# Moving the transposed scores one slot later and giving each value product its own slot in a fused FFN–attention–FFN kernel

## The chip, the cores and the metric

One core of one Trainium2 chip runs the whole kernel. The metric is the time of one execution on the device in microseconds (us). Lower is better.

## What is computed

The input X is 16 sequences of 256 rows by 128 columns. Three residual blocks follow each other:

```
x = x + 0.5 * ffn(layernorm(x))     # FP4-quantised activations and weights, 128 -> 352 -> 128, silu(gate) * up
x = x + attention(layernorm(x))     # 16 heads of 8, causal softmax, @ Wo + bo
x = x + 0.5 * ffn(layernorm(x))
```

In the attention, for each head, `A = softmax(Q K^T / sqrt(8), causal)` and `Y = A V`.

## The kernel before

**Stages.** The first FFN runs over the 16 sequences, then the attention, then the second FFN. Each is a software pipeline: iteration `it` (called a *turn* here) works on sequence `it - lag` at each step, by the table `ATT_LAG`, and all engines issue their share of the steps in the one order of `ATT_ORDER`. The attention has turns 0 to 22. Turns 0 to 4 are woven into the first FFN. Turns 5 to 7 and 16 to 19 are written out with the full order (`FULL`; in 18 and 19 the steps of sequences past the last fall away), turns 8 to 15 are a loop unrolled by four, and the rest, the tail, is woven by hand with the second FFN (`ATT_TO_FFN`, L113 to L124).

**Steps of one sequence.** `lnS lnA lnE lnN` is the layernorm (VectorE, GpSimd, then ScalarE). `xT`, copied by `xTc` (ScalarE, L754), is the transposed input; `qk` (TensorE, L1245) projects queries and keys. `c1`, `split`, `c2` and `third` cut them into three bf16 parts; `third` is a GpSimd subtraction (L604), `c2` a ScalarE cast (L764). `stack` stores the parts to DRAM and loads them back as stacks (SyncE's DMA queue). `v` is the value projection, copied by ScalarE (L772).

`S0` to `S11` (TensorE, L1268) are the scores, each one PSUM bank, and VectorE takes row maxima of each (L1050). `nmS` (VectorE, L1059 to L1065) splits the negated maxima in three parts. `nm` transposes them (TensorE, L1278), ScalarE copies them (L779), and a DMA puts them into the query stack (`load_nm`, L506).

`ST0` to `ST11` (TensorE, L1299) are the transposed scores with the maxima already subtracted. They alternate between the banks `st0` and `st1`. ScalarE takes the exponential of each (L790), GpSimd zeroes the upper triangle (the mask, L619). `ST0` waits for the DMA of the maxima. Three ST make up a group of four heads.

`AV0` to `AV3` (TensorE, L1326 and L1330, 128x32 weights, four heads side by side in the 128 columns) multiply one group each by the values. `AVg` waits for the mask of `ST(3g+2)`; the even ones also wait until the bank `ot0` is empty. `oc0` copies it after AV1, `oc1` after AV3 (ScalarE, L800). `oT0 oT1`, `n0 n1` (VectorE, L1073 and L1075), `yT`, `yTc` (ScalarE, L809), `wo` (TensorE, L1356) and `wa` normalise, transpose and project.

**Slots.** I call slot k of a turn the stretch of the order around `Sk`. One ST stands in each slot too. Each engine takes its steps strictly in the order, so a step that waits holds everything behind it on its engine.

The waits of the exponential and of the value product:

```python
if not first(b, 1):
    act.wait_ge(filled["AV"], GROUPS * (b - 1) + g + 1)          # exp(c): group's probs read by the sequence before
nc.scalar.activation(probs[:, c, :], ps[:, :], ACT.Exp, scale=SCALE).then_inc(done, 1)

pe.wait_ge(taken["AV"], PAIRS * b + pair)                        # attend(g), even g only
pe.wait_ge(masked, CHUNKS * b + 3 * g + 3)                       # attend(g), every g
```

Of the kernel before, what the change touches and what calls it, by code (L numbers as in the profile page):

```python
# [77 lines left out]
    "third stack v",  # L78
    "",
    "S0 S1 S2 S3 S4 S5 S6 S7 S8 S9 S10 S11",  # L80
    "nmS nm ST0 ST1 ST2 ST3 ST4",
    "ST5 ST6 ST7 ST8 ST9 ST10 ST11 AV0 AV1 AV2 AV3 oc0 oc1",
    "oT0 oT1 n0 n1 yT yTc wo wa sS sA sE",
)) for step in steps.split()}
ATT_ORDER = """
nmS ST5 S0 oT0 third  ST6 n0 S1  ST7 nm lnN S2 stack  ST8 S3 oT1 n1 AV0 AV1 bias
ST9 oc0 xT S4  ST10 xTc lnS S5 yT  yTc ST11 lnA S6  ST0 lnE S7 wo qk c1
ST1 wa S8  ST2 split S9 AV2 AV3  ST3 c2 oc1 sS S10 v  ST4 sA S11 sE
""".split()
ATT_UNROLL = 4  # L90
PART_TURNS = 2
# [16 lines left out]
FULL = " ".join(ATT_ORDER)  # L108
FFN_TO_ATT = [(13, None, FFN_TURN), (14, 0, WARM), (15, 1, WARM), (16, 2, WARM), (17, 3, WARM), (18, 4, FIRST_SCORES),
              (19, None, FIRST_REST), (20, None, REST_TRANSPOSES), (21, 4, REST_SCORES), (None, 1, "bias"), (None, 2, "bias"),  # L110
              (None, 3, "bias"), (None, 4, "bias"), (None, 5, FULL), (None, 6, FULL), (None, 7, FULL)]
LAST_PROBS = "nmS ST5 oT0 n0  ST6 nm f.xq  ST7 oT1  ST8  ST9 n1  ST10  ST11 AV0 yT f.xr"
LAST_RESIDUAL = "f.lnN  ST0  ST1 AV1 oc0 yTc  ST2 AV2  ST3  ST4 AV3 wo f.xq oc1 wa sS sA sE"  # L113
LAST_VALUES = """
ST5  ST6 f.xT  ST7 oT0 n0  ST8  ST9 AV0  ST10  ST11 f.xr f.gu0 AV1 f.gu1 oT1 n1 oc0 yT yTc AV2 AV3 f.h0 wo f.h1 wa oc1
"""
SECOND_GATES = "f.xT f.xq f.gu0 oT0 f.gu1 f.hq n0 f.xr f.h0 f.h1 f.hr f.lnN"
# [1 line left out]
THIRD_PRODUCTS = "f.xr f.h0 f.h1 f.hr f.lnN yT"  # L119
FOURTH_GATES = "f.hT0 f.xT f.hT1 f.xq f.gu0 yTc f.gu1 wo f.dn0 f.hq wa"  # L120
FOURTH_PRODUCTS = "f.xr f.h0 sS f.h1 sA sE f.hr f.lnN f.dn1"
ATT_TO_FFN = [(0, 16, FULL.replace("ST4", "f.lnN ST4")), (1, 17, FULL.replace("ST4", "f.lnN ST4")), (None, 18, FULL), (None, 19, FULL),
              (1, 20, LAST_PROBS), (2, 20, LAST_RESIDUAL), (2, 21, LAST_VALUES), (3, 22, SECOND_GATES),
              (4, 22, THIRD_GATES), (None, 21, "sS sA sE"), (4, 22, THIRD_PRODUCTS), (5, 22, FOURTH_GATES), (5, 22, FOURTH_PRODUCTS)]  # L124
VECTOR_COPIES = {"oc0": (14, 15), "oc1": (14,), "yTc": (13, 14), "f.xT": (0,)}
WOVEN_THIRDS = 3
# [116 lines left out]
def all_phases(eng, ffn1, att, ffn2, last, done=0):  # L243
# [5 lines left out]
    att.loop(eng)  # L249
    weave(ffn2, att, ATT_TO_FFN)  # L250
    ffn2.loop(eng)
# [6 lines left out]
def weave(ffn, att, turns):  # L258

    woven = set()
    for ffn_it, att_it, order in turns:
        for name in order.split():
            pipeline, it, step = (ffn, ffn_it, name[2:]) if name.startswith("f.") else (att, att_it, name)
            if it is not None and 0 <= it - pipeline.lag[step] < pipeline.batches:
                assert (pipeline is ffn, it, step) not in woven
                woven.add((pipeline is ffn, it, step))
                pipeline.step(step, it, it)
    for pipeline, n in ((ffn, 0), (att, 1)):  # L270
        for it in {turn[n] for turn in turns} - {None}:
            for step, lag in pipeline.lag.items():
                assert (pipeline is ffn, it, step) in woven or not 0 <= it - lag < pipeline.batches, (it, step)
# [1118 lines left out]
```

## Time and profile before

| | us |
|---|---|
| median of 3 runs | 486.52 |
| lowest, highest | 481.95, 491.36 |
| profiled execution, its own time | 480.36 |
| its span | 478.6 |
| TensorE busy | 390.8 (82%) |
| VectorE busy | 417.0 (87%) |
| ScalarE busy | 317.4 (66%) |
| GpSimd busy | 259.1 (54%) |

The profiled execution lies 6.2 us below the median. 1.8 us of it lie outside the span. The attention's full turns fill about 160 to 343 us of the span, the first FFN what lies before, the second what lies behind. Busy shares are averages over the three stages; a busy TensorE matmul row contains the latency of a pipelined matmul, so gaps between starts say more than busy time.

### The profile page before, as it was taken

The numbers are of one execution on the slowest core, as the hardware profiler recorded it, in microseconds if no ns is written. First come the engines' busy times: TensorE is split into PE (matmuls) and PEld (weight loads), VectorE is DVE, ScalarE is ACT, GpSimd is POOL, SyncE is SP. The second block draws the span as 40 slices with busy tenths as digits, with TensorE's granted clock in tenths as the row PEclk, the third lists the DMA queues.
The fourth block names the chain that finished last, engine by engine and source line by source line (L and its number), as shares of the span: only waits on it lengthen the run. The fifth ranks groups of instructions, "written<-read, shape, count | busy, mean of one in ns | idle before, by whom it ended". The sixth has DMA issues, their size and how long they took to land.

```text
span 478.6 us, 12396 instructions
## 1 busy us (share of the span) xinstructions
PE 390.8 (82%) x3433; PEld 285.9 (60%) x3433; DVE 417.0 (87%) x1132; ACT 317.4 (66%) x861; POOL 259.1 (54%) x479
## 2 busy tenths in 40 slices
PE   0558888887886899998999999988895778888886
PEld 0325665665574567676767767666553556656665
DVE  3788999998888879998999998878868999999994
ACT  3557888777651767777778777776773456656643
POOL 6455666645525457776777776656671242233321
PEclk9988999998899789999999999999999889999999
DMA  7887000000445444445554445440000000000001
GB/s 215 239 132 134 4 0 0 1 1 17 131 144 146 141 125 127 127 123 148 149 149 131 130 135 147 137 140 21 7 1 1 2 12 23 22 22 22 22 12 44
DMA packets 38440, 39.30 MB, mean 82 GB/s; under 512 B 1789, under 2 KB 35453, under 8 KB 36093
## 3 DMA queue, kind: packets, MB, share of 16 engines
q1 hardware_dynamic: 38397, 38.79, 30.5%
q8 instruction: 20, 0.33, 0.3%
q14 instruction: 23, 0.19, 0.1%
HBM read 21.91 MB, written 10.49 MB: 68 GB/s over the span
## 4 chain that ended last, share of the span: by engine, by line
PE 42%; issue 23%; DVE 10%; ACT 10%; POOL 8%; DMA 5%; POOLq 0%; ACTq 0%; DVEq 0%; SPq 0%
PE bank L1299 7%; PE bank L1326 6%; PE bank L1268 5%; DMA q_stack<-nmT 4%; PE bank L1159 4%; PE bank L1160 3%; PE bank L1188 3%; POOL hq_out L551 3%; PE bank L1245 3%; PE bank L1330 3%; ACT probs L790 2%; PE bank L1356 2%; POOL fln_rstd L577 1%; PE bank L1146 1%; PE bank L1179 1%
## 5 line engine op out<-in xcount | busy, mean ns | idle before, releaser
L1050 DVE TENSOR_REDUCE nm<-bank 128x2 f32<-128x512 f32 (+1 forms) x192 | 126.6, 682 | 20.6 <-PE bank L1268 18.3
L790 ACT ACTIVATE probs<-bank 128x512 f32<-128x512 f32 x192 | 108.7, 608 | 38.2 <-PE bank L1299 37.2
L619 POOL TENSOR_SCALAR_AFFINE_SELECT probs<-probs 128x256 f32<-128x256 f32 (+1 forms) x192 | 90.3, 485 | 59.0 <-ACT probs L790 56.9
L1299 PE MATMUL bank<-q_stack,k_stack 75*128 75x256 bf16 (+1 forms) x512 | 74.1, 248 | 9.8 <-ACT probs L790 5.0
L1268 PE MATMUL bank<-k_stack,q_stack 127*128 127x256 bf16 (+1 forms) x512 | 74.3, 250 | 1.5 <-DVE nm L1050 1.5
L551 POOL TENSOR_TENSOR xq_out<-xq_grid,xq_scale 128x256 f32<-128x256 bf16 x32 | 24.4, 762 | 76.5 <-DVE xq_grid L894 76.5
L1159 PE MATMUL bank<-wguT,f_xT 128*128 128x352 f32 x128 | 57.5, 534 | 6.3 <-ACT f_xT L713 4.3
L1299 PEld LDWEIGHTS bank<-q_stack,k_stack 75*128 75x128 bf16 x512 | 37.3, 97 | 29.4 <-ACT probs L790 13.7
L1188 PE MATMUL bank<-wdT,f_hT 128*128 128x128 f32 (+1 forms) x384 | 53.4, 275 | 1.4 <-ACT f_hT L731 1.4
L720 ACT ACTIVATE f_silu<-bank 128x352 f32<-128x352 f32 x64 | 29.3, 458 | 37.1 <-PE bank L1160 37.0
L1188 PEld LDWEIGHTS bank<-wdT,f_hT 128*128 128x128 f32 (+1 forms) x384 | 49.9, 191 | 6.5 <-ACT x_all L705 0.9
L1160 PE MATMUL bank<-wguT,f_xT 128*128 128x352 f32 x128 | 53.4, 501 | 0.0
L551 POOL TENSOR_TENSOR hq_out<-hq_grid,hq_scale 128x704 f32<-128x704 bf16 x31 | 42.8, 1382 | 10.8 <-DVE hq_grid L894 10.8
L1268 PEld LDWEIGHTS bank<-k_stack,q_stack 127*128 127x128 bf16 x512 | 41.2, 99 | 7.6 <-DVE nm L1050 2.9
L1146 PE MATMUL bank<-ident,xq_out 128*128 128x128 f32 x64 | 14.5, 311 | 37.5 <-POOL xq_out L551 22.2
L1326 PE MATMUL bank<-probs,v_stack 128*32 128x256 f32 x512 | 41.1, 393 | 0.2 <-DVE oT L1090 0.2
L1015 DVE TENSOR_TENSOR f_h<-f_silu,bank 128x352 f32<-128x352 f32 x64 | 32.6, 515 | 4.9 <-ACT f_silu L720 4.7
L1160 PEld LDWEIGHTS bank<-wguT,f_xT 128*128 128x128 f32 x128 | 26.9, 210 | 16.1 <-issue 4.5
L1159 PEld LDWEIGHTS bank<-wguT,f_xT 128*128 128x128 f32 x128 | 23.3, 208 | 20.7 <-ACT f_xT L713 14.3
L1179 PE MATMUL bank<-ident,hq_out 128*128 128x128 f32 (+1 forms) x192 | 32.4, 278 | 3.8 <-ACT f_hT L731 3.8
L1146 PEld LDWEIGHTS bank<-ident,xq_out 128*128 128x128 f32 x64 | 6.8, 146 | 45.8 <-POOL xq_out L551 26.9
L729 ACT COPY f_hT<-bank 128x256 f32<-128x256 f32 x64 | 23.8, 372 | 5.6 <-PE bank L1179 5.4
(149 smaller groups left out, 876.4 us busy)
## 6 DMA issues: line engine op xcount, KB each, us to landing
q_stack<-q_parts SPq DMA_DIRECT2D x16, 576.0 KB
k_stack<-k_parts SPq DMA_DIRECT2D x16, 576.0 KB
q_parts<-qk_parts SPq DMA_DIRECT2D x16, 192.0 KB, 2.1
k_parts<-qk_parts SPq DMA_DIRECT2D x16, 192.0 KB, 2.4
v_stack<-zeros_bf SPq DMA_DIRECT2D x1, 2048.0 KB, 10.1
k_parts<-qk_parts SPq DMA_DIRECT2D x16, 128.0 KB, 2.3
out_dram<-x_all SPq DMA_DIRECT2D x15, 128.0 KB, 1.8
q_stack<-mask_q SPq DMA_DIRECT2D x1, 1664.0 KB
```

The lines of the kernel that those rows point to most:

```text
L551: nc.gpsimd.tensor_tensor(q.out[:, s, :].rearrange("p (n k) -> p n k", k=BLOCK), q.grid[:, s, :].rearrange("p (n k) -> p n k", k=BLOCK), q ...
L619: nc.gpsimd.affine_select(out=v, in_=v, compare_op=ALU.is_ge, fill=0.0, base=0, pattern=[[0, heads], [1, P]], channel_multiplier=-1).then_ ...
L790: nc.scalar.activation(probs[:, c, :], ps[:, :], ACT.Exp, scale=SCALE).then_inc(done, 1)
L1015: nc.vector.tensor_tensor(f_h[:, j, :], f_silu[:, j, :], ps.up[j][:, 0:I], ALU.mult).then_inc(h_ready[j], 1)
L1050: nc.vector.tensor_reduce(nm[:, j, h0:h0 + n], ps[:, :].rearrange("p (h k) -> p h k", h=n), AX_X, ALU.max, negate=True).then_inc(done, 1)
L1159: nc.tensor.matmul(ps.gate[j][:, 0:I], x, wguT[:, 0, :], start=True, stop=True)
L1160: nc.tensor.matmul(ps.up[j][:, 0:I], x, wguT[:, 1, :], start=True, stop=True).then_inc(gu_filled[j], 1)
L1179: last = nc.tensor.transpose(ps.hT[0:k, P * t:P * t + P], hquant.out[:, s, I * j + P * t:I * j + P * t + k], ident[:, :])
L1188: nc.tensor.matmul(out, f_hT[0:k, t, P * j:P * j + P], wdT[0:k, t, :], start=(t == 0), stop=False)
L1268: last = nc.tensor.matmul(ps[:, keys * h:keys * h + keys], q_stack[0:ROWS, s, h0 + h, P * j:P * j + P], k_stack[0:ROWS, s, h0 + h, 0:keys] ...
L1299: last = nc.tensor.matmul(ps[:, w * n:w * n + w], k_stack[0:SROWS, s, HG * g + h, k0:k0 + P], q_stack[0:SROWS, s, HG * g + h, q0:T], start ...
L1326: nc.tensor.matmul(ps[VW * h:VW * h + VW, 0:T], window(s, 0, h), probs[:, slot + h // 2, T * (h % 2):T * (h % 2) + T], start=(half == 0), ...
```

## The change

All steps stay, with the same shapes, buffers and waits. Three things move:

- Every ST stands one slot later. Slot 0 now has ST4 and not ST5, and so on to slot 7 with ST11; ST0 stands in slot 8 and not 7, behind `wo`, `qk` and `c1`. ST4 moves to the lag of ST5.
- The value products stand alone: AV0 stays in slot 3, AV1 goes behind S4, AV2 behind S8, AV3 stays behind S9. `oc0` goes from slot 4 to slot 5, behind `xTc` and ahead of `yTc`.
- In the tail one more ST (ST4 of sequence 14) stands behind the last maxima; `LAST_RESIDUAL` is cut in two around ST4 of the last sequence, in the same order.

```diff
-    "nmS nm ST0 ST1 ST2 ST3 ST4",
-    "ST5 ST6 ST7 ST8 ST9 ST10 ST11 AV0 AV1 AV2 AV3 oc0 oc1",
+    "nmS nm ST0 ST1 ST2 ST3",
+    "ST4 ST5 ST6 ST7 ST8 ST9 ST10 ST11 AV0 AV1 AV2 AV3 oc0 oc1",
...
-nmS ST5 S0 oT0 third  ST6 n0 S1  ST7 nm lnN S2 stack  ST8 S3 oT1 n1 AV0 AV1 bias
-ST9 oc0 xT S4  ST10 xTc lnS S5 yT  yTc ST11 lnA S6  ST0 lnE S7 wo qk c1
-ST1 wa S8  ST2 split S9 AV2 AV3  ST3 c2 oc1 sS S10 v  ST4 sA S11 sE
+nmS ST4 S0 oT0 third  ST5 n0 S1  ST6 nm lnN S2 stack  ST7 S3 oT1 n1 AV0 bias
+ST8 xT S4 AV1  ST9 xTc oc0 lnS S5 yT  yTc ST10 lnA S6  ST11 lnE S7 wo qk c1
+ST0 wa S8 AV2  ST1 split S9 AV3  ST2 c2 oc1 sS S10 v  ST3 sA S11 sE
...
-LAST_PROBS = "nmS ST5 oT0 n0  ST6 nm f.xq  ST7 oT1  ST8  ST9 n1  ST10  ST11 AV0 yT f.xr"
-LAST_RESIDUAL = "f.lnN  ST0  ST1 AV1 oc0 yTc  ST2 AV2  ST3  ST4 AV3 wo f.xq oc1 wa sS sA sE"
+LAST_PROBS = "nmS ST4 ST5 oT0 n0  ST6 nm f.xq  ST7 oT1  ST8  ST9 n1  ST10  ST11 AV0 yT f.xr"
+LAST_SCORES = "f.lnN  ST0  ST1 AV1 oc0 yTc  ST2 AV2  ST3"
+LAST_RESIDUAL = "AV3 wo f.xq oc1 wa sS sA sE"
...
-ATT_TO_FFN = [(0, 16, FULL.replace("ST4", "f.lnN ST4")), (1, 17, FULL.replace("ST4", "f.lnN ST4")), (None, 18, FULL), (None, 19, FULL),
-              (1, 20, LAST_PROBS), (2, 20, LAST_RESIDUAL), (2, 21, LAST_VALUES), (3, 22, SECOND_GATES),
+ATT_TO_FFN = [(0, 16, FULL.replace("ST3", "f.lnN ST3")), (1, 17, FULL.replace("ST3", "f.lnN ST3")), (None, 18, FULL), (None, 19, FULL),
+              (1, 20, LAST_PROBS), (2, 20, LAST_SCORES), (None, 21, "ST4"), (2, 20, LAST_RESIDUAL), (2, 21, LAST_VALUES), (3, 22, SECOND_GATES),
```

## Rows read from the trace of the kernel before

**Rows 1.** The page: busy time, share, instructions.
```profile
PE 390.8 (82%) x3433; PEld 285.9 (60%) x3433; DVE 417.0 (87%) x1132; ACT 317.4 (66%) x861; POOL 259.1 (54%) x479
```
**Rows 2.** Chain that ended last, whole run: start, us, what (`qk`, turns 6, 8, 9, 16).
```profile
174.31 0.86 PE bank L1245 x4
...
199.55 0.87 PE bank L1245 x4
...
211.98 0.87 PE bank L1245 x4
...
301.07 0.87 PE bank L1245 x4
```
**Rows 3.** The same chain inside turns 8 and 9, ST3 to ST6.
```profile
202.74 0.34 PE bank L1299 x2
...
204.63 0.63 ACT probs L790
...
205.31 0.39 PE bank L1299 x2
```
**Rows 4.** Timeline of TensorE, turn 9: start, us, line, shapes [idle before].
```profile
207.38 0.64 PE L1326 MATMUL bank<-probs,v_stack 128*32 128x256 f32 x8
207.84 0.40 PE L1330 MATMUL bank<-probs,v_stack 128*32 128x128 f32 x8
208.06 0.61 PE L1326 MATMUL bank<-probs,v_stack 128*32 128x256 f32 x8
208.49 0.40 PE L1330 MATMUL bank<-probs,v_stack 128*32 128x128 f32 x8
208.82 0.39 PE L1299 MATMUL bank<-q_stack,k_stack 75*128 75x256 bf16 x2
...
210.97 0.39 PE L1268 MATMUL bank<-k_stack,q_stack 127*128 127x256 bf16 x2
211.30 0.68 PE L1356 MATMUL bank<-wqkvo,yT 128*128 128x128 f32 x4
```
**Rows 5.** Timeline of TensorE, turn 8, around AV2.
```profile
200.92 0.38 PE L1268 MATMUL bank<-k_stack,q_stack 127*128 127x256 bf16 x2
201.23 0.64 PE L1326 MATMUL bank<-probs,v_stack 128*32 128x256 f32 x8
```
**Rows 6.** Timeline of ScalarE, turn 9: exp of ST9, `oc0`, exp, `xTc`, `yTc`.
```profile
209.25 0.60 ACT L790 ACTIVATE probs<-bank 128x512 f32<-128x512 f32 x1 [0.84 <-PE bank L1299]
209.74 0.37 ACT L800 COPY oT<-bank 128x256 f32<-128x256 f32 x1
210.00 0.61 ACT L790 ACTIVATE probs<-bank 128x512 f32<-128x512 f32 x1
210.49 0.39 ACT L754 COPY a_xT<-bank 128x256 f32<-128x256 f32 x1
210.74 0.41 ACT L809 COPY yT<-bank 128x256 f32<-128x256 f32 x1
```
**Rows 7.** Timeline of GpSimd, turn 9: mask of ST5, `third`, masks of ST6 to ST8.
```profile
206.99 0.64 POOL L619 TENSOR_SCALAR_AFFINE_SELECT probs<-probs 128x512 f32<-128x512 f32 x1
207.59 1.17 POOL L604 TENSOR_TENSOR qk_parts<-qk_rest,qk_parts 128x512 bf16<-128x512 f32 x1
208.70 1.36 POOL L619 TENSOR_SCALAR_AFFINE_SELECT probs<-probs 128x256 f32<-128x256 f32 x3
```
**Rows 8.** Timeline of VectorE, turn 9: row maxima of S4.
```profile
209.69 0.69 DVE L1050 TENSOR_REDUCE nm<-bank 128x2 f32<-128x512 f32 x1 [0.45 <-PE bank L1268]
```
**Rows 9.** Waits: who for whom, us in total, times, longest us.
```profile
PE bank L1299 <- DMA q_stack<-nmT: 4.4, 5, 1.5
```
**Rows 10.** Timeline of TensorE, ST0 of turns 17 and 18.
```profile
314.25 0.38 PE L1299 MATMUL bank<-q_stack,k_stack 75*128 75x256 bf16 x2 [1.47 <-DMA q_stack<-nmT]
...
326.33 0.38 PE L1299 MATMUL bank<-q_stack,k_stack 75*128 75x256 bf16 x2 [0.71 <-DMA q_stack<-nmT]
```
**Rows 11.** Timeline of ScalarE in the tail: copy of the last sequence's maxima.
```profile
344.30 0.37 ACT L779 COPY nmT<-bank 48x256 bf16<-48x256 bf16 x1 [0.63 <-PE bank L1278]
```

## Prediction, made before the changed kernel was run

> **What bounds the kernel now.** I read the page first: VectorE is the busiest engine, 87%, TensorE 82% [rows 1]. That alone would make VectorE the bound, and the change would look like a relief for it, because its maxima of S4 wait 0.45 us each turn behind the pair AV0, AV1 [rows 8]. So I read the chain that ended last. It comes back to `qk` on TensorE in every turn, and from turn 6 to turn 16 it takes 301.07 - 174.31 = 126.76 us for ten turns [rows 2]. The undisturbed turn is 211.98 - 199.55 = 12.43 us [rows 2]. Ten of those are 124.3, so 2.46 us of the ten are disturbance.
>
> Inside a turn the chain leaves TensorE once: ST3 (202.74), its exponential, `c2`, `oc1`, `v`'s copy, the exponential of ST4 (204.63), and ST6, which needs that bank, at 205.31 [rows 3]. These 2.6 us are ScalarE's. The other 9.8 us are TensorE instruction behind instruction. VectorE isn't on the chain; its 0.45 us is slack.
>
> Disturbance comes from the DMA of the maxima: ST0 waited for it five times, 4.4 us together, 1.5 at most [rows 9]: 1.47 in turn 17, 0.71 in 18 [rows 10], the others in turns 6 to 16.
>
> **The change, part by part.** I walk through a turn with the gaps between starts of rows 4 to 7 and ask at each moved step what it now stands behind.
>
> *ST0 a slot later (gain).* Behind S7, `wo` and `qk` it runs some 1.9 us later (S7 at 210.97, `qk` at 211.98 and its 0.87 [rows 2, 4]), and the delays below add to it. The longest wait was 1.5 [rows 9], so all five go. In the ten turns that is 2.46 us. In 17 and 18 it is 1.47 + 0.71, less 0.1 or so that the next wait swallowed: 2.05. Together -4.5 us. Bounds: 0 if the load is late by something that moves along, -4.6.
>
> *Value products alone (loss).* A pair: AV0 takes 0.46 + 0.22 until AV1 starts, AV1 0.43 + 0.33 until ST9 starts [rows 4]. A score group of 256 columns otherwise starts 0.22 after the instruction before; so leaving the 128x32 products costs 0.11. Entering costs 0.09: S9 starts at 200.92, its two matmuls take 0.22, AV2 starts at 201.23 [rows 5]. The first group of a run takes 0.03 more. Each split adds one way in and one way out: 0.23 us. Two a turn, on the part of the chain that is TensorE's: 0.46. Over the 28 pairs of turns 6 to 19, 6.4 us. Bounds: 0, if the gaps are the price of AV's semaphore waits and the second of a pair, with one wait, has none; 28 x 0.33 = 9.2, if a split costs as much as the whole stretch from the last products to ST9. I take 0.23 because the way out shows at ST9, which has the one bank wait of every other ST.
>
 Without the rule the gaps could be waits and the term could be 0; the rule gives no duration.
>
> *AV1 behind `third` (loss).* AV1 needs the mask of ST5. Before, GpSimd did that mask (206.99) ahead of `third` (207.59) [rows 7]. Now the mask of ST4 stands there and the mask of ST5 behind `third`: 206.99 + 0.38 (ST4's mask, half as large) + 1.11 (`third`, 207.59 to 208.70) + 0.64 = 209.12, and 0.05 to TensorE, as from the exponential's end (204.63 + 0.63) to ST6 at 205.31 [rows 3]: 209.17. Without it AV1 would start at 207.38 + 0.79 (AV0 and the way out) + 3 x 0.22 (ST8, `xT`, S4) + 0.09 = 208.93. TensorE waits 0.24, and everything behind AV1 with it. `third` runs in turns up to 17: 11 x 0.24 = 2.6 us. Bounds: 0 (if ST4's mask and `third` start earlier) and 0.5 a turn.
>
> *`oc0` between ST9's exponential and `yTc` (loss).* On the scale without the wait of AV1, ST9 starts at 208.93 + 0.79 = 209.72. Its exponential starts 0.43 later (208.82 to 209.25 [rows 4, 6]), then 0.49, `xTc` 0.25, `oc0` 0.26 [rows 6]: `yTc` starts at 211.15, ends at 211.56, and `wo` can start at 211.61. TensorE would be there at 209.72 + 7 x 0.22 (ST9 to S7) + 0.11 (S7 at 210.97 to `wo` at 211.30, less 0.22 [rows 4]) = 211.37. It waits 0.24. Before, `yTc` ended at 211.15, ahead of `wo` at 211.30. Turns 7 to 16: 2.4. Turns 17 to 19 have no `xTc`, I take half: 0.4. Together 2.8 us. Bounds 0 and 0.35 a turn.
>
> *What stays.* The ScalarE stretch of 2.6 us begins at the ST of slot 10, which stands behind both AV2 and AV3 as before; its length is the same. S4 comes 0.7 us earlier; VectorE gains slack there that nobody waits for. At S9, one AV earlier in the queue than before, VectorE has `wa` and `split` to do. AV2 and AV3 wait for masks of slots 4 and 7, over a microsecond old. No DMA is added. `stack` waits for the last ST of four sequences earlier, now a slot later, but its stores release it later still.
>
> *Both ends.* Turn 5 loses one ST, 0.22 us, ahead of its maxima, at most; I count 0. In the tail one more exponential stands ahead of the copy of the last maxima; ScalarE was idle 0.63 us there [rows 11], an exponential is 0.5: 0.
>
> *Sum.* 6.4 + 2.6 + 2.8 - 4.5 = +7.3, less 0.3 for splits of turns 18 and 19 where VectorE may end the wait: +7.0. The full turn goes from 12.43 to 12.43 + 0.46 + 0.24 + 0.24 = 13.4 us, even in all turns. On the profiled execution's 480.36: 487.4 us.
>
> The median lies 6.2 us above that execution. In the trace, all unevenness of the turns is the load of the maxima, so I hold most of the 6.2 for more such waits, which go too. I let 0.6 us of them stand: **488 us**.
>
> **Rivals.**
>
> *The switches cost nothing.* If the gaps are semaphore waits, they fall away: 488 - 6.1 = 482 us. For it: `wo` too starts 0.11 late without a switch. Against: ST9 behind AV1, above.
>
> *The load of the maxima is the larger part, and the change is faster.* Place: ST0, every turn. In the median run these waits would be 4.5 + 6.2 = 10.7 us, all hidden now. With the other costs at 0 that gives 486.5 - 10.7 = 476; with a VectorE that was the bound after all, another 0.45 a turn for 13 turns, 470. It decides once the waits removed exceed the costs added by 9.7 us. For it: the spread of the runs, 481.95 to 491.36, and VectorE's 87%. Against: the order puts three new things behind queues, and the chain shows VectorE off it.
>
> *The waits add up.* All costs at their upper bounds: 9.2 + 11 x 0.5 + 13 x 0.35 = 19.3, less 4.5, is +15, and if the 6.2 us have nothing to do with the maxima: 486.5 + 15 = 501 us. Against: a wait on TensorE gives ScalarE and GpSimd time to catch up, so the two waits can't both be at their largest.
>
> **How the numbers follow.** Forecast 0.56, free switches 0.21, faster 0.10, adding up 0.13. The forecast has 484 to 494 for itself (0 or all of the 6.2 standing, and the mask wait at 0 or 0.5). With the free switches the range becomes **480 to 496**. A measurement of this kernel can tell about 2% from no change, 476.8 to 496.2 us. Faster by over 2%: 0.09, from its rival. Slower by over 2%: 0.15, from the waits that add up and a little of the forecast. Within 2%: 0.76.
>
> **What would show it.** Turns of 13.1 to 13.4 us, all alike; no wait of L1299 for the maxima; twice as many short idles before L1326; new waits of L1326 for the mask (L619) in slot 4 and of L1356 for `yT` (L809); VectorE's wait at S4 gone and its idle time elsewhere. Wrong would be turns below 12.43 (then VectorE was the bound), splits without gaps, or a wait at ST0 that stays.

## The result, and the profile after

| | before | after |
|---|---|---|
| median, executions side by side | 484.69 us (20) | 487.75 us (20) |
| lowest, highest | 481.74, 491.36 | 485.33, 489.65 |
| profiled execution, its span | 480.36, 478.6 | 488.02, 486.3 |
| `qk` of turn 6 to `qk` of turn 16 | 126.8 us | 133.6 us |

The changed kernel takes 1.0076 times the time of the kernel before, interval 1.0055 to 1.0097: slower by 0.8%, within the 2% and 0.25 us from the forecast. Medians here and below are over all executions; the ratios leave out those over 1.5% above the fastest of their kernel, which the kernel before has more often than the changed one, so a ratio can lie above the quotient of the medians. In the changed kernel's own line numbers every line named below is one higher than before.

The page of the changed kernel, busy time by engine, hardly differs from [rows 1]:

```profile
PE 396.6 (82%) x3433; PEld 282.2 (58%) x3433; DVE 416.6 (86%) x1132; ACT 319.8 (66%) x861; POOL 258.7 (53%) x479
```

The chain that ended last tells more. Its `qk` rows (start, us, what), turns 8 to 11:

```profile
197.76 0.87 PE bank L1246 x4
211.08 0.86 PE bank L1246 x4
224.40 0.87 PE bank L1246 x4
237.72 0.86 PE bank L1246 x4
```

A turn is now 13.32 us where it was 12.43 [rows 2]. Nine of the ten turns lie between 13.21 and 13.35 us; one is 13.79. Before, they went from 12.42 to 13.45.

TensorE's timeline of the changed kernel, turn 9 (start, us, line, shapes, [idle before]), from S4 to AV1, ST9 and on to S7, `wo`, `qk` and ST0:

```profile
207.08 0.38 PE L1269 MATMUL bank<-k_stack,q_stack 127*128 127x256 bf16 x2
207.62 0.64 PE L1327 MATMUL bank<-probs,v_stack 128*32 128x256 f32 x8 [0.15 <-POOL probs L620]
208.07 0.40 PE L1331 MATMUL bank<-probs,v_stack 128*32 128x128 f32 x8
208.41 0.39 PE L1300 MATMUL bank<-q_stack,k_stack 75*128 75x256 bf16 x2
...
209.74 0.39 PE L1269 MATMUL bank<-k_stack,q_stack 127*128 127x256 bf16 x2
210.40 0.68 PE L1357 MATMUL bank<-wqkvo,yT 128*128 128x128 f32 x4 [0.27 <-ACT yT L810]
210.91 1.03 PE L1246 MATMUL bank<-a_xT,wqk 128*128 128x256 f32 x4
211.78 0.38 PE L1300 MATMUL bank<-q_stack,k_stack 75*128 75x256 bf16 x2
```

AV1 starts 0.54 us after S4, where a value product behind scores starts 0.31 after them [rows 5]: 0.23 us is the wait for the mask behind `third`. `wo` starts 0.66 after S7, 0.33 before [rows 4]. ST0 follows `qk` without a gap. So a turn is 12.43 + 0.46 (two splits) + 0.23 (mask) + 0.33 (`yT`) - 0.14 (a gap that ST0 used to have) = 13.31 us.

ScalarE's timeline shows why `wo` waits: `oc0` (L801) stands between `xTc` and `yTc` (L810).

```profile
208.84 0.60 ACT L791 ACTIVATE probs<-bank 128x512 f32<-128x512 f32 x1 [1.18 <-PE bank L1300]
209.33 0.37 ACT L755 COPY a_xT<-bank 128x256 f32<-128x256 f32 x1
209.58 0.39 ACT L801 COPY oT<-bank 128x256 f32<-128x256 f32 x1
209.85 0.41 ACT L810 COPY yT<-bank 128x256 f32<-128x256 f32 x1
```

The waits of the changed kernel (who for whom, us in total, times, longest):

```profile
DVE nm L1051 <- PE bank L1269: 23.9, 48, 1.5
...
PEld bank L1327 <- issue: 8.3, 42, 0.2
PEld bank L1327 <- POOL probs L620: 6.0, 17, 0.6
...
PE bank L1357 <- ACT yT L810: 2.7, 10, 0.3
```

There is no row of a transposed score (L1300) waiting for the maxima's DMA, where before there was one of 4.4 us [rows 9].

**Where the 7.66 us between the two profiled executions went.** First FFN -1.15, turns 5 and 6 -1.96, the ten turns +6.81, the rest of the attention +0.42, the first turns of the second FFN +3.58, all else -0.04. The +6.81 and the +0.42 are where the attention's order moved; the others are taken up behind the experiments.

### The profile page after: what moved, and what is told of

The parts are those of the page before. It is cut to its first block, busy times and chain, and to the rows that moved or that the text cites. A ratio compares the mean times of both kernels' runs of the same rounds, so it can differ in the third digit from the quotient of the medians.

```text
span 486.3 us, 12396 instructions
## 1 busy us (share of the span) xinstructions
PE 396.6 (82%) x3433; PEld 282.2 (58%) x3433; DVE 416.6 (86%) x1132; ACT 319.8 (66%) x861; POOL 258.7 (53%) x479
## 4 chain that ended last, share of the span: by engine, by line
PE 41%; issue 24%; ACT 12%; DVE 10%; POOL 10%; ACTq 1%; DMA 1%; POOLq 1%; DVEq 0%
PE bank L1300 7%; PE bank L1327 6%; PE bank L1160 4%; PE bank L1269 4%; PE bank L1161 3%; PE bank L1189 3%; POOL hq_out L552 3%; PE bank L1246 3%; ACT probs L791 3%; PE bank L1331 2%; PE bank L1357 2%; ACT oT L801 2%; PE bank L1147 1%; POOL probs L620 1%; POOL fln_rstd L578 1%
## 5 line engine op out<-in xcount | busy, mean ns | idle before, releaser
L1051 DVE TENSOR_REDUCE nm<-bank 128x2 f32<-128x512 f32 (+1 forms) x192 | 127.5, 684 | 25.3 <-PE bank L1269 23.9
L791 ACT ACTIVATE probs<-bank 128x512 f32<-128x512 f32 x192 | 109.9, 606 | 41.3 <-PE bank L1300 40.8
L1300 PE MATMUL bank<-q_stack,k_stack 75*128 75x256 bf16 (+1 forms) x512 | 74.1, 249 | 7.1 <-ACT probs L791 7.0
L1300 PEld LDWEIGHTS bank<-q_stack,k_stack 75*128 75x128 bf16 x512 | 35.5, 98 | 28.8 <-ACT probs L791 13.4
L1327 PE MATMUL bank<-probs,v_stack 128*32 128x256 f32 x512 | 40.9, 391 | 1.8 <-POOL probs L620 1.4
L872 DVE SCALAR_TENSOR_TENSOR hq_normed<-f_h,hq_inv 128x704 f32<-128x704 f32 x31 | 27.3, 880 | 0.1
```

Source lines behind the costliest of these rows:

```text
L1051: nc.vector.tensor_reduce(nm[:, j, h0:h0 + n], ps[:, :].rearrange("p (h k) -> p h k", h=n), AX_X, ALU.max, negate=True).then_inc(done, 1)
L1300: last = nc.tensor.matmul(ps[:, w * n:w * n + w], k_stack[0:SROWS, s, HG * g + h, k0:k0 + P], q_stack[0:SROWS, s, HG * g + h, q0:T], start ...
L1327: nc.tensor.matmul(ps[VW * h:VW * h + VW, 0:T], window(s, 0, h), probs[:, slot + h // 2, T * (h % 2):T * (h % 2) + T], start=(half == 0), ...
```

## The experiments

"Turn" is the undisturbed turn, "ten turns" the time from `qk` of turn 6 to `qk` of turn 16, "load waits" those of ST0 on the maxima's load over the whole run, turns 17 and 18 included. The ratio is to the kernel before, timed side by side (its medians there were 483.45 to 485.61), and is what compares kernels of different rows. No ratio is 2% away from 1, though the intervals of x1, x3 and y3 reach past that; where an interval contains 1, no difference is shown. A turn's time counts from its `qk` to the next. Each trace is one execution.

| kernel | turn | ten turns | load waits | median | ratio |
|---|---|---|---|---|---|
| before | 12.43 | 126.75 | 4.4 | | 1 |
| changed | 13.32 | 133.57 | 0 | 487.75 | 1.0076 [1.0055, 1.0097] |
| x1_extra_waits | - | 133.64 | 12.4 | 485.77 | 1.0118 [0.9981, 1.0256] |
| x2_split_only | 12.80 | 132.38 | 3.9 | 483.82 | 1.0009 [0.9959, 1.0058] |
| x3_third | 13.09 | 131.69 | 2.0 | 487.33 | 1.0129 [1.0027, 1.0231] |
| x4_ytc | 13.04 | 130.82 | 0 | 484.14 | 1.0028 [0.9972, 1.0083] |
| x5_third_ytc | 12.81 | 129.64 | 4.5 | 486.37 | 1.004 [0.9994, 1.0086] |
| x6_pairs | 12.85 | 132.15 | 5.8 | 490.23 | 1.0114 [1.0047, 1.0182] |
| x7_c2 | 12.85 | 131.75 | 5.8 | 487.46 | 1.0052 [1.0011, 1.0093] |
| x8_c2_nm | 13.33 | 135.09 | 0 | 487.07 | 1.0062 [1.0023, 1.0101] |
| y1_wait_moved | 12.43 | 126.09 | 1.2 | 480.7 | 0.9874 [0.981, 0.9938] |
| y2_after_wait | 13.32 | 133.59 | 0 | 486.15 | 1.0071 [1.0045, 1.0097] |
| y3_pairs_wait | 12.48 | 125.52 | 0 | 477.85 | 0.9844 [0.9788, 0.99] |
| y4_pairs_xt | 12.48 | 130.19 | 6.6 | 486.24 | 1.0036 [0.9996, 1.0077] |

### Are the gaps around the value products waits?

**x1_extra_waits**, the kernel before with satisfied semaphore waits added:

```diff
+    if half == 1:
+        if not first(b, 1):
+            pe.wait_ge(taken["AV"], PAIRS * b)
+        pe.wait_ge(taken["v"], b + 1)
     pe.wait_ge(masked, CHUNKS * b + 3 * g + 3)
...
     if c == 0:
         pe.wait_ge(nm_loaded, 16 * (b + 1))
+    if c in (3, 9):
+        pe.wait_ge(nm_loaded, 16 * (b + 1))
```

> The kernel before, with two more waits that are already satisfied ahead of AV1 and AV3 and one more ahead of ST3 and ST9; order and work are the same. Theory (the gaps round the 128x32 products are the change of tiling, not the price of waits): AV1 still starts 0.22 us behind AV0's last products, ST9 still 0.33 behind AV1's, the undisturbed turn stays at 12.43 us (at most +0.1), ratio to before 1.000 within 0.003. Rival (the gaps are what semaphore waits cost): about 0.1 us more ahead of AV1 and AV3 and behind AV3 and AV1, so +0.3 to +0.5 us a turn and +4 to +6 us in all, ratio 1.008 to 1.013.

Measured, on TensorE's timeline of this kernel:

```profile
259.20 0.64 PE L1332 MATMUL bank<-probs,v_stack 128*32 128x256 f32 x8
259.65 0.40 PE L1336 MATMUL bank<-probs,v_stack 128*32 128x128 f32 x8
259.87 0.61 PE L1332 MATMUL bank<-probs,v_stack 128*32 128x256 f32 x8
260.30 0.40 PE L1336 MATMUL bank<-probs,v_stack 128*32 128x128 f32 x8
260.64 0.39 PE L1301 MATMUL bank<-q_stack,k_stack 75*128 75x256 bf16 x2
```

AV0's last group to AV1 is 0.22 us and AV1's last group to ST9 0.34, as in [rows 4] (0.22 and 0.33). Satisfied waits cost nothing there. The gap belongs to the change between 128x32 weights and the others. The element type, which changes at the same places, is not it: `v` (fp32) starts 0.22 us behind a bf16 score (203.12 behind 202.90 in the kernel before), and in the later y3_pairs_wait `xT` (fp32, 128x128) starts 0.34 behind the fp32 products of AV1 (216.91 behind 216.57).

The time itself says little. The ratio, 1.0118, lies where the rival had it, but its interval contains 1, and the medians are 485.77 and 485.32. The turn of 12.43 could not be read, since ST0 waited for the load in nine of the ten turns (turn 6, without a wait, took 12.54 us in both kernels); the profiled execution has three times the load waits of the kernel before, whose order it shares.

**x2_split_only**, the kernel before with AV1 behind S4, AV2 behind S8, and `oc0` behind `yTc`; no transposed score moves.

```diff
-nmS ST5 S0 oT0 third  ST6 n0 S1  ST7 nm lnN S2 stack  ST8 S3 oT1 n1 AV0 AV1 bias
-ST9 oc0 xT S4  ST10 xTc lnS S5 yT  yTc ST11 lnA S6  ST0 lnE S7 wo qk c1
-ST1 wa S8  ST2 split S9 AV2 AV3  ST3 c2 oc1 sS S10 v  ST4 sA S11 sE
+nmS ST5 S0 oT0 third  ST6 n0 S1  ST7 nm lnN S2 stack  ST8 S3 oT1 n1 AV0 bias
+ST9 xT S4 AV1  ST10 xTc lnS S5 yT  yTc oc0 ST11 lnA S6  ST0 lnE S7 wo qk c1
+ST1 wa S8 AV2  ST2 split S9 AV3  ST3 c2 oc1 sS S10 v  ST4 sA S11 sE
```

> The kernel before with the value products apart (AV1 behind S4, AV2 behind S8, AV3 behind S9) and oc0 behind yTc, where it holds up nothing; the transposed scores stay in their slots, so AV1's mask is ahead of the third parts and ST0 still stands ahead of wo. Theory: each split costs 0.23 us, the turn goes from 12.43 to 12.9 us, no waits of AV1 for the mask or of wo for yT, the waits of ST0 for the maxima stay (a little shorter, as ST0 comes 0.23 later behind them): +5 to +6.4 us, ratio 1.010 to 1.013. In turn 6 TensorE idles as before and its clock falls as before. Rival (splitting is free or helps, as VectorE's wait at S4 goes): the turn is 12.4 or shorter, ratio 0.99 to 1.000.

The turn is 12.80 = 12.43 + 0.46 - 0.10: both splits at 0.23, and a gap ahead of ST0 that shrank from 0.14 to 0.04. The Trainium skill (TensorEngine Tiling (Array Packing), Key Properties) says that a change of tiling mode drains the engine. The trace agrees in so far as each change has a gap, 0.23 us for the way in and out together; that the gap is a drain is not shown apart.

Two expectations failed. The whole time did not rise by 5 to 6.4 us: the ratio is 1.0009 with an interval of 0.9959 to 1.0058. And the clock in turn 6 did not fall. Both are taken up below.

### The two waits of the changed kernel

**x3_third** and **x4_ytc** are the changed kernel with one step moved each, x3 by the first pair of lines, x4 by the second.

```diff
-nmS ST4 S0 oT0 third  ST5 n0 S1
+nmS ST4 S0 oT0  ST5 third n0 S1
...
-ST9 xTc oc0 lnS S5 yT  yTc ST10
+ST9 xTc lnS S5 yT  yTc oc0 ST10
```

> The changed kernel with third one step later, behind ST5 and not ahead of it, so that GpSimd masks ST5 before it subtracts. Theory: AV1's wait for the mask goes, the turn goes from 13.32 to 13.09 us, -2.6 us over 11 turns, 485 us beside 487.75 for the changed kernel. Rival (the mask wait only hid another wait, for yT): AV1 starts earlier but wo waits so much longer, the turn stays 13.32 and the time 487.75.

> The changed kernel with oc0 behind yTc and not ahead of it. Theory: wo's wait of 0.33 us goes, the turn goes from 13.32 to 13.0 us, -3.5 us, 484 us. Rival (oc0 later makes AV2 wait for its bank, or the exponentials for ScalarE): the turn stays above 13.2, and AV2 shows a wait for oT's copy.

The turns are 13.09 and 13.04: 0.23 and 0.28 us come back. The median of x4 is the 484 us expected; that of x3, 487.33 over four executions, does not show the 2.6 us. **x5_third_ytc** has both:

> The changed kernel with both small repairs at once: the third masks moved from slot 4 (ahead of ST5) to behind ST5, and the copy yTc moved ahead of oc0 on ScalarE; the four value products stay apart. My theory (independent costs on TensorE's path, each of which comes back alone): an undisturbed turn of the attention stage is 13.32 us in the changed kernel, 13.09 with the third alone and 13.04 with yTc alone, so both give 13.32 - 0.23 - 0.28 = 12.81 us, ten turns from qk(6) to qk(16) take 133.6 - 5.1 = 128.5 us. Rival (the two repairs share a cover: once one wait is gone, VectorE's chain of maxima ends next): the turn stops at 12.95 us or more. Against the kernel before (ten turns 126.75 with its waits on the maxima's load of this profile): 128.5 + 0.4 - 1.2 = about 1 us more, ratio 1.000 to 1.005 in favour of the changed side, or 0.5 to 1% less time where the kernel before meets more of its load waits.

The turn is 12.81, so the costs add up exactly. But the ten turns took 129.64, not 128.5, and load waits were back in a kernel whose ST0 has the later slot: 0.4 us of them in the ten turns, 0.4 in turn 16 and 3.7 in turns 17 and 18.

### Only the later slot

**x6_pairs** also puts the pairs together again (AV0 AV1 behind S4, AV2 AV3 behind S9).

```diff
-ST6 nm lnN S2 stack  ST7 S3 oT1 n1 AV0 bias  ST8 xT S4 AV1  ST9
-ST0 wa S8 AV2  ST1 split S9 AV3
+ST6 nm lnN S2 stack  ST7 S3 oT1 n1 bias  ST8 xT S4 AV0 AV1  ST9
+ST0 wa S8  ST1 split S9 AV2 AV3
```

> The kernel of the run before with the value products in pairs again (AV0 AV1 behind S4, AV2 AV3 behind S9): what remains of the change is only that the transposed scores stand one slot later behind the maxima. My theory: the two splits taken back give 2 x 0.23 = 0.46 us a turn, so an undisturbed turn is 12.81 - 0.46 = 12.35 us, all turns even (no wait of a transposed score on the maxima's load), ten turns 124 us, some 10 us less than the changed kernel's 133.6 and some 2.7 less than the 126.75 of the profiled kernel before, more against executions with larger load waits: ratio to the kernel before 0.98 to 0.99. Rival A (the pairs wait for their masks, since AV1 now stands only half a slot behind ST8): 0.2 to 0.3 us a turn come back, turn 12.6. Rival B (the load wait is worth nothing, since something else sets the turn): the turn is 12.43 with uneven turns as in the kernel before, ratio 1.00.

None of the three came out. The turn is 12.85. Of the missing 0.5 us some 0.36 is a wait of `xT` (the rest was not followed): without AV0 ahead of it, it reaches the norm's output (`lnN`, ScalarE L662) while that is being written, ten times and 3.6 us in all. One of them:

```profile
274.00 0.44 PE L1237 MATMUL bank<-ident,aln_out 128*128 128x128 f32 x2 [0.31 <-ACT aln_out L662]
```

And the load waits are larger than before, up to 2.0 us in the ten turns, with turns of 15.05 and 14.05, and 2.5 in turn 17. The kernel with the cheap turn is no faster than the changed one (ratios 1.0114 and 1.0076, with intervals that overlap). This broke my picture of the load, and SyncE's timeline shows why. In x6_pairs (start, us to issue, line, transfer), around the wait of turn 12:

```profile
243.50 0.76 SPq L499 DMA_DIRECT2D q_stack<-zeros_bf  x1
245.05 0.77 SPq L507 DMA_DIRECT2D q_stack<-nmT  x1
252.12 0.38 SPq L489 DMA_DIRECT2D q_parts<-qk_parts  x1
...
257.31 0.77 SPq L499 DMA_DIRECT2D q_stack<-zeros_bf  x1
259.38 0.74 SPq L507 DMA_DIRECT2D q_stack<-nmT  x1
265.50 0.37 SPq L489 DMA_DIRECT2D q_parts<-qk_parts  x1
```

and the two ST0 that waited, on TensorE's timeline:

```profile
252.22 0.39 PE L1300 MATMUL bank<-q_stack,k_stack 75*128 75x256 bf16 x2 [2.03 <-DMA q_stack<-nmT]
...
266.27 0.39 PE L1300 MATMUL bank<-q_stack,k_stack 75*128 75x256 bf16 x2 [1.02 <-DMA q_stack<-nmT]
```

The maxima's load takes 7.17 and 6.89 us from its own issue, where the chain of the kernel before shows 3.6 to 4.6 in the ten turns. From the issue of `zeros_bf` (24 KB), the last of the three transfers into the stacks ahead of it, it is 8.72 and 8.96. The kernel before has the same:

```profile
215.87 0.76 SPq L498 DMA_DIRECT2D q_stack<-zeros_bf  x1
219.73 0.75 SPq L506 DMA_DIRECT2D q_stack<-nmT  x1
223.71 0.38 SPq L488 DMA_DIRECT2D q_parts<-qk_parts  x1
```

```profile
224.37 0.39 PE L1299 MATMUL bank<-q_stack,k_stack 75*128 75x256 bf16 x2 [1.18 <-DMA q_stack<-nmT]
```

224.37 is 4.64 us after the maxima's load and 8.50 after `zeros_bf`. Over the 31 waits of ST0 in turns 6 to 16 of eight kernels, ST0 starts 7.9 to 9.3 us after `zeros_bf`, while the maxima's load was issued 1.5 to 4.6 us after it. I read this as follows: the small load (24 KB) lands when the two stack loads of 576 KB ahead of it in the queue are through, whenever it is issued itself. The Trainium skill (DMA: Bandwidth & Descriptors, Queues, rings and completion order) says that SyncE's queue has one ring on each of the DMA engines, that descriptors there are consumed in ring order, and that a transfer's semaphore increment lands only after every earlier write of the same DMA engine. By that rule a small transfer has to let a large one ahead of it through; the trace agrees with the 8.5 us. No run put the small load on another queue, so that it is the order in the queue, and not the DMA engines that both use, is argued.

The third row of each group shows the next sequence's stores (`q_parts<-qk_parts`), issued 7.8 to 8.6 us after `zeros_bf`. In `stack` the code has them behind a wait for the stack loads of the sequence before. From the stores to the next `zeros_bf` it is 5.13 to 5.19 us (252.12 to 257.31). That closes a loop of transfers (us):

stores (5.15) -> stack loads (about 8) -> next stores.

Where ST0 waits for it, it has a period of its own: 13.38, 12.88, 13.14 and 13.48 us in x6_pairs from 252.12 on; 13.25 in the mean of seven in x1_extra_waits; 12.59 in the mean of six in the kernel before, where only two of these turns have a wait. TensorE's turn of 12.43 is shorter, so the loads fall behind by the difference each turn until ST0 waits. A later slot moves the point where ST0 begins to wait; it does not shorten the loop.

### Two more edits to x6_pairs

**x7_c2** moves `c2` behind ST3 (first pair of lines); **x8_c2_nm** also moves `nm` and `lnN` one slot later (second pair).

```diff
-ST2 c2 oc1 sS S10 v  ST3 sA S11 sE
+ST2 oc1 sS S10 v  ST3 c2 sA S11 sE
...
-ST6 nm lnN S2 stack  ST7 S3
+ST6 S2  ST7 nm lnN stack S3
```

> The kernel of the run before (pairs, both repairs) with ScalarE's copy c2 moved from slot 2, behind ST2, to slot 3, behind ST3. My theory: in the slots without it ScalarE's run of exponentials ends 0.2 us sooner and TensorE's wait for it shrinks by up to 0.15 us a turn: turn 12.2 to 12.35. Rival: VectorE's chain of maxima is nearly as long and takes the place of that wait: the turn stays at 12.35 within 0.05.

> The kernel of the run before with the step nm and the norm lnN moved one slot later (behind ST7 instead of ST6). It asks how close the maxima's load is to ending the turn once the transposed scores stand a slot later: nm starts about 1.1 us later. My theory: the changed kernel has over 1 us of slack between the landing of the load and ST4 (its profile shows no wait there at all), and VectorE's work around nm is merely reordered, so the turn stays within 0.1 us of the run before or gains up to 0.3 where VectorE's norm no longer stands ahead of S2's maximum. Rival: the slack is under 1 us and the load ends the turn again: waits of the transposed scores on the load come back in several turns and the turn grows by 0.3 to 1 us.

x7 keeps the turn of the run before, 12.85, in kind as its rival had it. In x8 neither expectation came out: the norm's output comes later with `nm`'s copy ahead of it, and `xT` waits for it 12 times, 7.6 us in all; the turn grows to 13.33. With a turn above the loop's period no ST0 waited for the load, though that load was issued half a us later. (Turn 8 of x8 took 14.95 us with no such wait; TensorE's granted clock was 0.50, its lower level of 1.2 GHz, from 209 to 211 us there, after `xT` had waited.) What decides, by these runs, is the turn against the loop.

### Opening the loop

The stores need not wait for the loads of the sequence before; only the next loads must. **y1_wait_moved** is the kernel before with that one wait moved:

```diff
     wait_apart(sp, parts3_ready, b + 1, passed_sp)
-    if not first(b, 1):
-        wait_apart(sp, stacks_loaded, 16 * N_LOADED * b, passed_sp)
...
     wait_apart(sp, parts_stored, 16 * N_STORED * (b + 1), passed_sp)
+    if not first(b, 1):
+        wait_apart(sp, stacks_loaded, 16 * N_LOADED * b, passed_sp)
```

> The kernel before with one wait moved: the step stack has the wait for the landing of the turn before's stack loads ahead of the stores of the parts; here it stands behind the stores, ahead of the loads. New theory (a loop of transfers): the maxima's load stands in SP's queue behind the two stack loads of 576 KB and lands 8.0 to 9.2 us after the last of them is issued, whenever it is issued itself; the next turn's stores wait for that landing, and the next loads for the stores, so that stores, loads and landing close a loop with a period of its own of 12.1 to 13.6 us (13.0 in the mean), which sets the turn wherever TensorE's own turn is shorter. With the wait moved the stores start when the third parts are ready (3.06 us ahead of qk instead of 1.5), the loads 1.5 us sooner, and the loop is shorter by the stores: no wait of ST0 on the maxima's load, turns of 12.43 but for single disturbed ones, ten turns 124.5 to 125.5 us, ratio to the kernel before 0.980 to 0.990, since its median holds more of these waits than its profiled execution. Rival A (the transfers themselves are slow): the stores now run beside the loads, both get slower, waits of 4 us or more in ten turns stay, ratio 1.00 or above. Rival B (the load's latency varies by chance, 3.3 to 4.7 us from its own issue): no change, ratio 0.995 to 1.005.

SyncE's timeline of this kernel:

```profile
260.24 0.38 SPq L486 DMA_DIRECT2D q_parts<-qk_parts  x1
...
265.51 0.77 SPq L498 DMA_DIRECT2D q_stack<-zeros_bf  x1
271.12 0.73 SPq L506 DMA_DIRECT2D q_stack<-nmT  x1
272.66 0.38 SPq L486 DMA_DIRECT2D q_parts<-qk_parts  x1
```

The stores now go out 7.15 us after `zeros_bf`, 12.42 us after the stores before, and 2.9 to 3.1 us ahead of `qk` in every turn from 11 on, where it was 1.4 to 2.1 in the kernel before: they go with the turn, no longer with the loads. The maxima's load is issued 5.6 us after `zeros_bf`, where it was 4.0 to 5.0 in the kernel before's later turns. `qk` in the chain:

```profile
250.94 0.87 PE bank L1245 x4
263.36 0.87 PE bank L1245 x4
275.79 0.87 PE bank L1245 x4
288.22 0.86 PE bank L1245 x4
```

Six of ten turns are 12.42 or 12.43, one load wait of 1.2 us is left (turn 9), and the kernel is 1.3% faster by the ratio (0.9874, at most 0.9938; six executions), 1.0% by the medians. The ten turns, 126.09, are above the 124.5 to 125.5 expected, by turn 9 (13.49) and turn 11 (12.80, as in the kernel before). In the profiled executions this is only 0.7 us less than before, and as a whole they took the same, 480.30 and 480.36 us. The gain stands in the other executions. That the kernel before loses more to the loop there than in its profiled one is the likely reason; it has no second trace that would show it. Rival A and rival B are both out. The one edit touches no order and no work.

**y2_after_wait** is the changed kernel with the same wait moved.

> The changed kernel with the same wait moved behind the stores. Theory of the loop of transfers: TensorE's turn of 13.32 us is longer than the loop's period in nearly all turns, so the changed kernel has nothing to gain: undisturbed turn 13.3, ten turns 133 to 133.6 us, ratio to the kernel before 1.003 to 1.010 as the changed kernel itself (1.0076). Against the kernel before with the wait moved it is then 8 to 9 us slower: the whole price of the splits and of the third masks and yTc, with nothing set against it. Rival (the changed kernel too is held by transfers): its turns get shorter than 13.2.

Nothing moved: 13.32, 133.59, ratio 1.0071 against 1.0076. With the loop open in both, the change costs 133.59 - 126.09 = 7.5 us in the ten turns. Of the whole time it costs 5.45 us by the medians and 2.0% by the ratios (1.0071 / 0.9874), some 9.6 us; the 8 to 9 expected lie between.

**y3_pairs_wait** and **y4_pairs_xt** are the later slot with everything else mended, with the wait moved (y3) and with the wait where it was (y4):

```diff
-nmS ST4 S0 oT0 third  ST5 n0 S1  ST6 nm lnN S2 stack  ST7 S3 oT1 n1 AV0 bias
-ST8 xT S4 AV1  ST9 xTc oc0 lnS S5 yT  yTc ST10 lnA S6  ST11 lnE S7 wo qk c1
-ST0 wa S8 AV2  ST1 split S9 AV3  ST2 c2 oc1 sS S10 v  ST3 sA S11 sE
+nmS ST4 S0 oT0  ST5 third n0 S1  ST6 nm lnN S2 stack  ST7 S3 oT1 n1 bias
+ST8 S4 AV0 AV1 xT  ST9 xTc lnS S5 yT  yTc oc0 ST10 lnA S6  ST11 lnE S7 wo qk c1
+ST0 wa S8  ST1 split S9 AV2 AV3  ST2 c2 oc1 sS S10 v  ST3 sA S11 sE
```

> The transposed scores a slot later as in the changed kernel, with the third masks behind ST5, yTc ahead of oc0, the value products in pairs, xT behind the first pair (in the kernel with pairs TensorE waited 0.36 us a turn for the norm's output, which n1 writes only just ahead of xT), and the wait of the stores moved. Theory: the undisturbed turn of the kernel with pairs was 12.85; without the wait for the norm it is 12.4 to 12.6, and the loop of transfers no longer holds it: ten turns 124 to 126 us, ratio to the kernel before 0.98 to 0.99, the same as the kernel before with the wait moved within 0.5%. Then the later slot of the transposed scores is worth nothing by itself once the loop is open. Rival (the later slot is worth its 1.1 us of slack beside the loop): it is faster than the kernel before with the wait moved by over 0.5%.

> The kernel of the run before (transposed scores a slot later, pairs, xT behind the first pair, third masks and yTc mended) with the wait of the stores put back ahead of them, where the kernel before and the changed kernel have it. It asks whether the later slot alone, in a turn that TensorE could do in 12.48 us, gets rid of the wait for the maxima's load. Theory (loop of transfers with a period of 12.8 to 13.5 us): no. The slot buys 1.1 us once, the loads fall behind by 0.3 to 1 us a turn, and from the fourth or sixth of the ten turns on the transposed scores wait for the maxima's load again: gap between the last stack load and the maxima's load down from 4.6 to under 2.5 us, ten turns 128 to 132 us, ratio to the kernel before 0.995 to 1.010, and 1.5 to 2.5% slower than the same kernel with the wait moved. Rival (one slot is enough, as the changed kernel's profile with no such wait suggests): turns even at 12.48, ten turns 125.5, ratio 0.984 as with the wait moved.

Both have a turn of 12.48. (What the first expectation puts on `n1` is `lnN`'s.) With the wait where it was, seven waits for the load, 2.7 us at most, came back from the fifth of the ten turns on, the longest in turn 17; two rows of the waits (y4_pairs_xt, then the kernel y1_wait_moved):

```profile
PE bank L1300 <- DMA q_stack<-nmT: 6.6, 7, 2.7
```

```profile
PE bank L1299 <- DMA q_stack<-nmT: 1.2, 1, 1.2
```

y4 loses 4.7 us in the ten turns against y3, and stands at 1.0036 against 0.9844. y3 is the fastest kernel of the study: 1.6% faster than the kernel before (1.0 to 2.1% by the interval), and against y2, timed beside it, 1.7% by the medians and 2.3% by the ratios. Against y1 its ratio is 0.9844 to 0.9874 with intervals that overlap (0.6% by the medians, six executions each), so whether the later slot is worth anything once the loop is open stays open; it is at most small.

## Why the prediction was right, and which step of it was not

The number (488.0 for 487.75), the sign and the turn (13.4 for 13.32) came out. That the number fits to 0.25 us is partly luck. It was added to a base of 486.52, the median of three executions, which is 484.69 over twenty: 1.5 us of loss were forecast and 3.1 measured. In the profiled executions +7.0 was forecast and +7.66 measured; there the attention's +6.81 and +0.42 are the forecast's terms, and -1.15, -1.96 and +3.58 have nothing to do with them and nearly cancel. Step by step:

**Value products alone, +0.46 a turn: right**, by x2 (0.46) and x1 (not the waits). "The switches cost nothing" is refuted.

**AV1 behind `third`, +0.24: right**, 0.23 in the timeline and in x3.

**`oc0` ahead of `yTc`, +0.24: under-sized.** 0.33 in the timeline, 0.28 back in x4. The start of `yTc` came out as reckoned. What was wrong is the 0.05 us from its end to `wo`: in the timelines above `yTc` ends at 210.26 and `wo` starts at 210.40, 0.14 later, and it is 0.13 to 0.15 in every undisturbed turn of the changed kernel and of x4, where `wo` still starts 0.38 behind S7; so only 0.28 of the 0.66 came back. It is 0.15 in the kernel before too (211.15 to 211.30, [rows 4, 6]), so the 0.11 that `wo` starts late there is already a wait for `yTc`. The prediction read `yTc` as ahead of `wo`, and counted the 0.11 for the rival of the free switches.

**The gap of 0.14 ahead of ST0 that disappeared: not in the sum.** It more than made up for the missing 0.09. ST0 takes the bank of ST10, whose exponential ends at 210.61 in the kernel before, with `oc0` ahead of it [rows 6]; ST0 starts at 210.74 there, 0.13 later. In x2, where `oc0` stands behind, that exponential ends earlier against TensorE, and ST0 again starts 0.13 after its end (249.69 to 249.82), with a gap of 0.04 or 0.05. So it was a wait for that exponential.

**ST0 a slot later, "so all five go", -4.5: right in the traces, wrong in its reason.** The step set the longest wait, 1.5 us, against 1.9 us of later issue, as if the load had a latency of its own. By the 31 waits it ends with the stack loads, and these run in a loop whose period lies above TensorE's turn of 12.43 us. y4 has the later slot and 6.6 us of these waits. In the changed kernel they are gone because its turn of 13.32 us lies above the loop's period, that is, because of the very costs that the other steps add. The bound that I named and put aside, "0 if the load is late by something that moves along", was the true one for a kernel with a cheap turn. Had the change had no splits, the same reasoning would have forecast a gain, and x6_pairs (1.0114) and y4_pairs_xt (1.0036) show that there is none.

Not all of the 2.46 us was load either: turns 6, 7 and 11 hold 0.75 of it and no load wait. Turn 11 is the longer one in y3 too (12.84 for 12.48) and in the changed kernel (13.79 for 13.32), where no ST0 waits for the load at all.

The true price of the reordering is therefore what y1 and y2 show, some 7.5 us in the ten turns. In the pair that was asked about, part of it is hidden, since the kernel before spends time waiting for the loop anyway. x2 shows the same: its splits cost 0.46 us a turn, and its time did not rise measurably.

**The 6.2 us of the median as more load waits: partly borne out, the size not shown.** Over twenty executions it is 4.3 us, not 6.2. x1_extra_waits, with the order of the kernel before, speaks for load waits: it had 12.4 us of them in its profiled execution of 486.21 us, and the same loop took 12.59 us a turn in one execution and 13.25 in the other. The rival "the load is the larger part" was right that more is to be had there than the profiled execution shows: y1 is 1.3% faster. It was wrong that this change gets it. The spreads fit: 4.3 us over 20 executions of the changed kernel and 2.7 over 12 of y2, whose turn lies above the loop's period, 9.6 over 20 of the kernel before.

But TensorE's clock spreads with the time, which the prediction left out. Over the 82 executions of the kernel before that stood beside the experiments, the mean granted clock goes from 0.950 to 0.979 of full speed; the nine executions at 0.974 or more took 481.2 us in the mean, the fourteen at 0.955 or less 488.9. In the changed kernel it only goes from 0.964 to 0.972. How much of the spread is waits, how much clock, and how much of the lower clock comes from the waits themselves, no run separates. The gain of y1 does not hang on it: set against a straight line through those 82, each of its six executions is 4.3 to 7.4 us faster than the kernel before at the same clock.

**The ends at 0: right for the change, wrong for the pair of executions.** The windows of the kernel before, then of the changed one (us; busy time and instructions by engine; granted clock; DMA share; GB/s), for turn 6 and for the start of the second FFN:

```profile
168.00:176.00 8.00, 7.98 (x82) 5.50 (x81) 5.35 (x13) 5.04 (x12) 4.01 (x10) 0.79 0.34 91
...
372.00:380.00 8.00, 5.15 (x22) 3.18 (x21) 7.74 (x25) 3.95 (x11) 3.15 (x5) 0.89 0.00 1
```

```profile
168.00:176.00 8.00, 7.97 (x99) 5.53 (x98) 6.27 (x14) 5.52 (x13) 5.31 (x13) 1.00 0.53 151
...
372.00:380.00 8.00, 5.42 (x13) 3.20 (x14) 7.54 (x25) 1.40 (x4) 2.15 (x3) 0.57 0.00 0
```

The granted clock was 0.79 and 1.00 of full speed in turn 6, and 0.89 and 0.57 in the second FFN. These are means over its two levels, 1.2 and 2.4 GHz (0.50 and 1.00). In windows of one us the kernel before is at 0.50 from 169 to 172 us, after TensorE had been busy 0.32 and 0.07 of the two us from 166 to 168. In the second FFN it is at 0.50 first for some 3 us (from 370.3 on, TensorE idle from 366.0 to 370.5), the changed kernel for some 7 (from 372.4 on, idle from 370.1 to 374.3).

x1_extra_waits, with the old order, had 1.00 and 0.57 as the changed kernel has, and y2, with the order of the changed kernel, again 1.00 and 0.57. The first four turns of the second FFN took 31.8 us in the kernel before, 34.7 in x1, 35.4 in the changed kernel and 34.4 in y2. So the -1.96 and most of the +3.58 us need no cause in the change; 0.7 us of the latter is more than x1 shows, and less than the 1.0 by which the two executions of the changed order differ. The -1.15 in the first FFN was not followed.

**What would show it.** Even turns, no load wait, 42 short issue gaps ahead of L1327 where there were 27, the new waits of AV1 and `wo`, VectorE's wait at S4 gone and its idle elsewhere (23.9 us in 48 for 18.3 in 27): all there. That each sign appeared did not prove the reason behind the fourth step; only a kernel with the later slot and a short turn could.

**Open.** Even y1 spreads from 474.9 to 485.8 us over six executions, so the loop is not the only thing that varies. Why the loop takes 12.6 us in one execution and 13.3 in another was not found, nor why once or twice in each trace the loads go out 1.2 to 2 us later than 5.15 behind the stores, nor what makes turn 11 longer. Whether the maxima's load would land sooner on a queue of its own was not tried. The cause of the gap ahead of ST0 is read from the traces; no run tested it by itself.

## What to carry to other kernels

When an instruction waits for a small transfer, measure its landing from the issue of the large transfers ahead of it in the queue, not only from its own; if that number is the constant one, the wait most likely belongs to them. Then look for what those wait for in turn: a closed loop of stores, loads and waits has a period of its own, and slack given to the consumer is used up within a few turns if the period is above the turn. Take a wait for completion out of the loop (here by moving it behind the stores, 1.3%) before reordering compute around it, and keep products of one weight shape together.

## What the runs showed of the hardware

- A load of 24 KB stands on the same queue behind two loads of 576 KB and a third of 24 KB. Issued 1.5 to 4.6 us behind that third one, it released its waiter 7.9 to 9.3 us after the third was issued, in each of 31 waits.
- From the end of a ScalarE copy (`yTc`) to the start of the TensorE product that waits for it (`wo`) it took 0.13 to 0.15 us.
- Entering and leaving the 128x32 products costs 0.09 and 0.11 us, 0.03 more for the first group: 0.23 us for each split, at a granted clock of 1.00. Two satisfied semaphore waits added ahead of AV1 and one ahead of ST9 left their starts at 0.22 and 0.34 us.
- The granted clock of TensorE at the start of the second FFN was 0.89 over 8 us in one execution and 0.57 in another of the same order of work (the kernel before and x1_extra_waits), and 0.79 or 1.00 in turn 6.
